# Edge passes of a four-layer graph network: a group's narrow one-hots built by one VectorE operation that compares broadcasts

## What is computed

```python
x = x + L0(h, edge_index)   # per edge |h[dst] - h[src]|, summed by node, then linear layers
x = x + L1(h, edge_index)   # two attention layers with 8 heads: softmax over the edges into a node
x = x + L2(h, src, dst)     # GraphConv: D^-1/2 A D^-1/2 h @ W, relu
x = x + L3(h, edge_index)   # two GCN layers, a sigmoid
```

## Time and profile before

| | before |
|---|---|
| median of 3 runs | 6823.97 us |
| lowest, highest | 6818.98, 6826.37 us |
| span of the profiled execution | 6821.1 us (no other time of it is shown) |
| TensorE matmul, busy | 5330.0 us (78%) |
| VectorE, busy | 4417.1 us (65%), 13076 instructions |
| ScalarE, busy | 2947.5 us (43%) |
| GpSimd, busy | 3074.8 us (45%), 3096 instructions |
| chain that ended last | PE 41%, DVE 30%, issue 13%, DMA 6% |

### The profile page before, as it was taken

The page is one execution under the profiler, slowest core; times in us unless marked ns, Lnnn a source line. Parts: engine busy times, 40 slices in busy tenths (PEclk is TensorE's granted clock), DMA queues, the critical chain, the costliest instruction groups (busy, mean ns, idle before and its releaser), DMA issues.

```text
span 6821.1 us, 123603 instructions
## 1 busy us (share of the span) xinstructions
PE 5330.0 (78%) x28313; PEld 3580.4 (52%) x28314; DVE 4417.1 (65%) x13076; ACT 2947.5 (43%) x5602; POOL 3074.8 (45%) x3096
## 2 busy tenths in 40 slices
PE   6987995777877656666676767776767999999998
PEld 3443443666666545555554556655655444444433
DVE  8999997788787468888886578888886111000000
ACT  1552551777777325666665335555553000000000
POOL 2763772777777006777774027777770000000000
PEclk9999996999999868999997878888888999999999
DMA  1000001555555306777776026666671677777799
GB/s 24 0 3 1 0 0 56 180 181 181 179 180 176 63 30 194 222 222 224 225 221 153 10 91 202 206 206 204 206 185 45 246 288 286 273 285 289 305 424 384
DMA packets 464533, 1168.30 MB, mean 171 GB/s; under 512 B 112062, under 2 KB 175102, under 8 KB 432156
## 3 DMA queue, kind: packets, MB, share of 16 engines
q1 hardware_dynamic: 337228, 892.75, 35.3%
q0 software_dynamic: 124928, 273.12, 16.2%
q10 hardware_dynamic: 2256, 0.89, 0.1%
HBM read 759.86 MB, written 405.30 MB: 171 GB/s over the span
## 4 chain that ended last, share of the span: by engine, by line
PE 41%; DVE 30%; issue 13%; DMA 6%; DVEq 5%; ACT 3%; POOL 1%; ACTq 0%; SPq 0%; POOLq 0%
PE PS L1085 17%; PE PS L787 6%; DVE ACC L1747 5%; DMA ACC<-adj 3%; DVE SCR L1800 3%; PE PS L811 3%; DVE SCR L1785 3%; PE PS L896 2%; PE PS L916 2%; DVE Q L1541 2%; PE PS L914 2%; PE PS L918 2%; DVE ITEM L1755 2%; PE PS L926 2%; DVE Q L1539 2%
## 5 line engine op out<-in xcount | busy, mean ns | idle before, releaser
L720 POOL DMA_INDIRECT ACC<-tab_kv,STAGE x1664 | 1639.7, 985 | 1231.9 <-DMA STAGE<-IDX 703.2
L926 PE MATMUL PS<-ITEM 128*128 128x512 f16 x1456 | 596.3, 410 | 581.6 <-ACT PS L1244 579.9
L1244 ACT ACTIVATE PS<-PS,X 128x512 f32<-128x512 f32 x1456 | 964.4, 662 | 180.4 <-PE PS L926 120.9
L720 POOL DMA_INDIRECT SCR<-tab_h,STAGE x832 | 806.9, 970 | 317.7 <-issue 195.7
L1747 DVE TENSOR_TENSOR ACC<-ACC,PS 128x137 f32 (+1 forms) x2288 | 749.1, 327 | 210.5 <-PE PS L918 75.3
L1085 PE MATMUL PS<-ACC,Q 128*128 128x512 f32 (+3 forms) x2548 | 840.9, 574 | 46.5 <-DMA ACC<-adj 35.8
L896 PE MATMUL PS<-Q,SCR 128*128 x4992 | 744.3, 296 | 91.2 <-issue 90.2
L787 PE MATMUL PS<-Q 128*128 128x416 f16 x4160 | 757.0, 340 | 61.2 <-DVE Q L1541 61.2
L896 PEld LDWEIGHTS PS<-Q,SCR 128*128 128x128 f32 x4992 | 691.1, 207 | 206.4 <-issue 183.2
L681 POOL DMA_INDIRECT placed<-ACC,X x576 | 606.2, 1052 | 410.1 <-DVE X L1518 221.5
L914 PE MATMUL PS<-SCR 128*128 128x137 f32 x3328 | 571.1, 321 | 189.9 <-DVE ACC L1747 189.9
(11 more groups left out here) (297 smaller groups left out, 7519.8 us busy)
## 6 DMA issues: line engine op xcount, KB each, us to landing
ACC<-adj SPq DMA_DIRECT2D x252, 1792.0 KB, 6.8
adj<-X SPq DMA_DIRECT2D x936, 256.0 KB
adj<-ITEM SPq DMA_DIRECT2D x520, 256.0 KB
ACC<-tab_kv,STAGE POOLq DMA_INDIRECT x1664
SCR<-tab_h,STAGE POOLq DMA_INDIRECT x832
tab_kv<-SCR SPq DMA_DIRECT2D x14, 896.0 KB, 4.1
ACC<-adj SPq DMA_DIRECT2D x21, 448.0 KB, 3.9
placed<-ACC,X POOLq DMA_INDIRECT x576, 2.3
```

Of the source, the lines that this page charges most:

```text
L720: nc.gpsimd.indirect_dma_start(G[:, q, j, 0:w], None, table, bass.IndirectOffsetOnAxis(STAGE[:, u, q * S4 + j:q * S4 + j + 1], 0))\
L926: nc.tensor.matmul(CLASS_SUM[k % 2], OHS1[:, k % ring, :], OHD[:, k % ring, :], start=False, stop=True, skip_group_check=True).then_inc(ad ...
L1244: nc.scalar.activation(CLASS_SUM[(k + 1) % 2], CLASS_SUM[k % 2], ACT.Copy, scale=KEEP[:, bass.ds(i, 1)])\
```

## The change

A function `item_rows` builds the narrow one-hots of all the items of a group (three or two) with one two-tensor comparison, IOTA512's first 128 columns broadcast over the items against LOK's columns broadcast over 128 elements. `item` keeps only the wide one. The wait for the ring slot is made once, for the last item of the group, ahead of the new operation; it is left out where the last item is still in the ring's first turn.

```diff
+                def item_rows(items):
+
+                    (i, k, ring), n = items[0], len(items)
+                    assert k % ring + n <= ring
+                    last = i + (n - 1)
+                    if not isinstance(last, int) or last >= PLAN[name][0] + ring:
+                        dve.wait_ge(ad["summed"], last - (ring - 1))
+                    V.tensor_tensor(OHS1[:, k % ring:k % ring + n, :], over_tiles(IOTA512[:, 0:P], n),
+                                    over_features(LOK[:, bass.ds(i, n)]), ALU.is_equal)
+
                 def item(i, k, ring):
 
-                    first = PLAN[name][0] + ring
-                    if not isinstance(i, int) or i >= first:
-                        dve.wait_ge(ad["summed"], i - (ring - 1))
-                    V.tensor_scalar(OHS1[:, k % ring, :], IOTA512[:, 0:P], LOK[:, bass.ds(i, 1)], None, ALU.is_equal)
                     V.tensor_scalar(OHD[:, k % ring, :], IOTA512[:, :], DREL[:, bass.ds(i, 1)], None, ALU.is_equal)\
                         .then_inc(ad["built"], 1)
...
                         if exists(gi + 1):
+                            item_rows(next_items(name, it, u))
                             for each in next_items(name, it, u):
                                 item(*each)
...
                         ahead = next_items(name, it, u) if exists(gi + 1) else []
+                        if ahead:
+                            item_rows(ahead)
                         for each in ahead[0:1]:
                             item(*each)
                         wait(dve, s, "ex", gi + 1)
...
+                item_rows(items_of(name, 0, 0))
                 for each in items_of(name, 0, 0):
                     item(*each)
```

## The result

| | before | after |
|---|---|---|
| median of 4 runs each | 6821.48 us | 6877.03 us |
| lowest, highest | 6817.46, 6826.37 us | 6876.13, 6879.27 us |
| span of the profiled execution | 6821.1 us | 6877.5 us |
| VectorE, busy | 4417.1 us | 4435.1 us |

The change makes the kernel slower: ratio 1.0084, 95% interval 1.0070 to 1.0099. The time lies 47 us above the forecast of 6830 and 15 above the range.

The account below looks back on a forecast made before the run. GpSimd's gathers were taken to bound the difference and second attention passes, VectorE's sequence the first attention pass. VectorE's -8 and GpSimd's +14 gave +6 on the runs' median of 6823.97, so 6830 us, range 6800 to 6862.

Parts of the forecast that it names:

- The bound: GpSimd's gathers pace the difference and second attention passes; VectorE's own sequence bounds the first, GpSimd 2% behind.
- the forecast's sign: Period of a group in the first attention pass: 5.25 to 5.30 us if the forecast holds.
- The engine price of the form: New operation on VectorE: recorded about 0.42 and 0.55 us; start to start 0.34 and 0.47; +6 us of engine time.
- The form's hold on the gathers: GpSimd term: gathers starting in the longer new operation wait; +14 us in all, ends 0 and +134.
- The failed step: Attention passes: the message product starts 0.18 or 0.31 us later, and the next group's first addition still follows; no cost.
- The term of -8 in the first attention pass: VectorE's shorter group tail less the later message product: -2 to -14 us, taken as -8.
- Slower: the port: Rival: one gather of a group stays just behind the new operation's start; 6840 to 6870, value 6850; chance 0.27.
- Doesn't run as written: Rival: mixed 16-bit and 32-bit broadcast inputs make the new operation take two cycles an element; 6890 and more; chance 0.04.
- durations in full: Rival: the narrow one-hots' recorded durations count in full, -99 us where VectorE bounds; 6725; chance 0.04.
- the issue: Rival: VectorE's sequencer tail shortens by the larger values and gathers meet fewer locks; 6802; chance 0.17.
- Cheaper narrow one: Rival: the 0.16 us step is the sequencer's, so each narrow one-hot removed frees 0.05 less; 6856; chance 0.03.
- The merged wait: Single wait for the ring slot of the group's last item, ahead of the new operation: costed at nothing.

Follow-up runs that it names:

- e3: Kernel before with the message product moved ahead of all item one-hots in both attention passes, old narrow comparisons kept: 6813 us, ratio 0.9989 to before.
- e2: Kernel before with all old narrow comparisons, one by one, ahead of the first wide one in the attention passes, no merged operation: 6855 us, ratio 1.0049.
- e9: Kernel before with the message product ahead of the item one-hots in the first attention pass alone, old comparisons kept: 6798 us, ratio 0.9969.

## Why the prediction was wrong

**The bound: right in two passes, half right in the third.** GpSimd's gathers were named as the bound in the difference and the second attention pass, with 0.11 us a group of slack in the first. In the changed kernel that slack goes first (GpSimd's waits in that pass fall from 22 to 9 us); the period there became 900/669 x 4 = 5.38 us, beyond the 5.25 to 5.30 given as the forecast's sign. But the bound of that pass was not the length of VectorE's sequence, as written: e3 has the same operations in it, and the pass is 21 us shorter, since the product frees the buffers earlier.

**The engine price of the form: right.** Recorded 0.42 and 0.55 us, the wide one-hot 0.08 before its end. The forecast of VectorE's busy time, down by 100 us, was wrong: it rose by 18. The recorded durations did fall by 99 (387.7 to 289.0), but busy time is a union, and the narrow ones had overlapped their neighbours.

**The form's hold on the gathers: right in kind, a third too small.** +14 was forecast. In the difference pass +9 was measured where 10.6 - 4 stood; in the attention passes 11 where 6.9 stood, the first one's share being costed as absorbed by slack. The new operation itself holds gathers for 41 us, against 28 in the working. The mean gather rose by 0.013 us in the difference pass, the forecast's mark (0.01 to 0.02), and by 0.028 in the attention passes, between that and the port case's (0.05).

**The failed step** is this one: "The message product frees the gather buffers and feeds TensorE's sums; 0.18 to 0.31 later, the next group's first addition still comes after them". It priced the later product for TensorE and VectorE, as nothing, and not for GpSimd. The product is a two-tensor operation of 0.68 us, the same kind and length as the one in the earlier trace rows whose hold I had just read. Before, it held 9 gathers; pushed later it holds 197. By e2 that step is worth about +35 us; nothing stood for it in the sum of GpSimd, and the moved work entered the total as VectorE's -8 alone. Rows of before could have told it: the earlier trace rows with GpSimd's line beside it have a gather that starts 0.11 ahead of the product's end, just free. I counted the delays of the operations that the change adds, not of those that it moves.

**The term of -8 in the first attention pass** also failed by its own working. The tail did shorten (in the two-item group of the second pass shown above, the opening follows the last wide one-hot's start at 4311.66 by 0.57, with 0.20 idle), but in the first pass the product came 0.31 later in most two-item groups too (62 of 102), where 0.18 was written. The missing 0.13 is the wide one-hot ahead of it, as at 4310.03: 0.47 us long in the median of those groups instead of 0.35, since it now falls into the late part of a running gather. The earlier trace rows showed one such (0.48), unread.

**The rivals.** "Slower: the port" (0.27) had the mechanism: gathers fall behind a long operation's start and stay there in group after group. It named only the new operation and gave 6850; with the product's share it is 6877. "Doesn't run as written" is out by the durations, "durations in full" and "the issue" by the sign. "Cheaper narrow one" no run tests; the longer gathers leave no loss for it. The merged wait, costed at nothing, costs next to nothing.

## What to carry to other kernels

When GpSimd gathers set the pace, price a VectorE edit by where gathers start against the long two-tensor operations, those it adds and those it moves. Look at the gather behind a held one first: its start follows the holding operation's end by a fixed time (1.13 us here), so it repeats group after group and can stand a hundredth of a microsecond from the next hold. A hundred gathers held for 0.25 us each outweigh all that merging small operations can save. Short operations hold next to nothing, so four short ones and one long one aren't interchangeable at equal engine time. And every removed hold shifts the next gathers: measure an edit pass by pass, and keep its order only in the passes where it wins, as e9 does.

## What was not expected of the hardware

The hold works in one direction for some operations and in both for others. Two-tensor operations are never stretched: step one-hot and product average 0.68 to 0.69 us at whatever point of a running gather they start. One-scalar operations are. Counted over the trace of before, to the nearest tenth, a wide one-hot that starts 0.5 to 0.6 us into a gather takes 0.45 to 0.47 on average, at the other points 0.35 (0.39 at 0.7); a narrow one 0.32 to 0.34 instead of 0.25 (0.28 at 0.7). I had cited the Trainium skill, "SBUF — State Buffer", section "SBUF: two separate sides", by which whoever starts first holds the shared ports for the whole instruction. The runs agree that there is a hold and differ in its extent: of the 236 gathers of before that start in the last 0.13 us of the step one-hot or the product none is held, and a gather holds a one-scalar operation in a late part of itself alone.

The second surprise is how far a local move reaches. The 0.19 us of four short operations for a long one cost 150 us over 624 groups, 0.24 a group, more than the engine time they add.
